# One Silu over both halves of the gate, one Softplus over both halves of dt, in a Mamba and 1-bit convolution kernel

## The reference, cut to what matters

```python
xz = jnp.einsum('bld,ed->ble', x, W_in)
xc, z = jnp.split(xz, 2, axis=-1)
xt = conv_general_dilated(jnp.transpose(xc, (0, 2, 1)), conv_w, ...)   # 4 taps, per channel
xc = silu(jnp.transpose(xt, (0, 2, 1)) + conv_b)
dbc = jnp.einsum('ble,re->blr', xc, W_x)                               # 8 rows of dt, 16 of B, 16 of C
dt = softplus(jnp.einsum('blr,er->ble', dbc[..., :8], W_dt) + b_dt)
# for each step: h = exp(dt * A) * h + (dt * xc) * B;   y = sum over states of h * C
y = (y + xc * D_skip) * silu(z)
return jnp.einsum('ble,de->bld', y, W_out)
```

## Time and profile before

| | us |
|---|---|
| median of 3 runs | 813.15 |
| lowest and highest run | 813.04, 813.65 |
| the profiled execution | 812.14 |
| its span | 810.3 |

### The profile page before, as it was taken

One profiled execution on the slowest core, in us unless ns is written; L12 is line 12 of the kernel. 1 busy time (PEld: TensorE's weight loads), 2 busy tenths in 40 slices (PEclk: granted clock), 3 DMA queues, 4 the chain that ended last, 5 costly groups with the idle time before them and its releaser, 6 DMA issues.

```text
span 810.3 us, 13741 instructions
## 1 busy us (share of the span) xinstructions
PE 740.5 (91%) x4854; PEld 403.1 (50%) x4854; DVE 727.1 (90%) x488; ACT 724.0 (89%) x1358; POOL 690.5 (85%) x211
## 2 busy tenths in 40 slices
PE   8798989898989898998989898989898997899998
PEld 5544444444444444544444544444544444557876
DVE  4799999999999999999999999999999999995141
ACT  5899999999999999999999999999999999865050
POOL 0579999999999999999999999999999999970000
PEclk9999999999999999999999999999999999999999
DMA  7817071726252433516161616253533525000011
GB/s 209 299 32 267 12 248 53 243 86 224 78 200 103 181 123 124 205 58 234 31 232 56 243 57 225 105 202 100 186 117 113 191 59 198 35 2 1 0 40 66
DMA packets 40173, 106.05 MB, mean 131 GB/s; under 512 B 8012, under 2 KB 11176, under 8 KB 40104
## 3 DMA queue, kind: packets, MB, share of 16 engines
q1 hardware_dynamic: 38476, 104.87, 37.2%
q10 hardware_dynamic: 1628, 0.30, 0.2%
HBM read 102.01 MB, written 3.15 MB: 130 GB/s over the span
## 4 chain that ended last, share of the span: by engine, by line
PE 34%; ACT 31%; DVE 14%; issue 11%; POOL 8%; DMA 2%; ACTq 1%; POOLq 0%; DVEq 0%; SPq 0%
PE bank L1261 11%; ACT product L772 10%; DVE state L1030 9%; PE bank L1547 8%; ACT bank L741 6%; ACT state L752 6%; PE bank L1254 5%; PE bank L1240 5%; POOL state L648 3%; POOL state L659 3%; DVE bank L1030 3%; PE bank L1365 2%; ACT xc L787 2%; ACT L860 2%; ACT L870 1%
## 5 line engine op out<-in xcount | busy, mean ns | idle before, releaser
L659 POOL TENSOR_TENSOR state<-state,wide 128x2048 f32<-128x2048 f32 (+1 forms) x104 | 408.1, 3956 | 5.4 <-DVE state L1030 5.4
L648 POOL TENSOR_TENSOR state<-u,wide 128x1024 f32<-128x1024 f32 (+1 forms) x77 | 249.1, 3259 | 25.3 <-DVE state L997 24.3
L1261 PE MATMUL bank<-state,ident 64*64 64x512 f32 x2048 | 250.1, 601 | 7.4 <-POOL state L659 7.4
L772 ACT ACTIVATE product<-u_tok,b_tok 128x256 f32<-128x256 f32 x588 | 248.0, 499 | 3.0 <-PE bank L1254 2.9
L1030 DVE TENSOR_TENSOR_SCAN state<-bank,state 128x1024 f32<-128x1024 f32 x109 | 246.7, 2276 | 3.3 <-ACT bank L741 2.2
L752 ACT ACTIVATE state<-dt,a_neg 128x512 f32<-128x512 f32 x294 | 193.0, 711 | 0.0
L1254 PEld LDWEIGHTS bank<-ident,product 128*128 128x128 f32 x1176 | 129.4, 141 | 121.0 <-issue 100.2
L1254 PE MATMUL bank<-ident,product 128*128 128x128 f32 x1176 | 156.0, 276 | 27.8 <-DVE state L1030 19.9
L1030 DVE TENSOR_TENSOR_SCAN bank<-state,bank 128x1024 f32<-128x1024 f32 x77 | 173.9, 2277 | 3.0 <-PE bank L1254 3.0
L1030 DVE TENSOR_TENSOR_SCAN state<-state,bank 128x1024 f32<-128x1024 f32 x70 | 158.4, 2267 | 3.2 <-PE bank L1254 3.2
L741 ACT ACTIVATE bank<-dt,a_neg 128x512 f32<-128x512 f32 x218 | 140.7, 677 | 0.9 <-DVE state L1030 0.2
(11 more groups left out here) (103 smaller groups left out, 469.0 us busy)
## 6 DMA issues: line engine op xcount, KB each, us to landing
wide<-bc_rows SPq DMA_DIRECT2D x159, 512.0 KB, 5.8
wide<-bc_rows SPq DMA_DIRECT2D x47, 256.0 KB, 3.9
x_t<-in_x_dram SPq DMA_DIRECT2D x4, 512.0 KB, 6.0
out_dram<-x_t SPq DMA_DIRECT2D x8, 256.0 KB, 2.0
k_room<-in_L_conv_w_dram SPq DMA_DIRECT2D x2, 576.0 KB, 6.7
bc_rows<-dbc SPq DMA_DIRECT2D x32, 32.0 KB, 1.5
state<-in_L_conv_W_in_dram SPq DMA_DIRECT2D x2, 256.0 KB, 3.8
x_tok<-in_x_dram ACTq DMA_DIRECT2D x1, 256.0 KB, 3.7
```

Of the source, the lines that this page charges most:

```text
L648: pool.tensor_tensor(tiles(group), u_for(len(group)), rows(b_wide, PLAIN.index(s), len(group)), ALU.mult).then_inc(plain_input, 1)
L659: pool.tensor_tensor(tiles(group), tiles(group), rows(c_wide, group[0] % NST, len(group)), ALU.mult).then_inc(output_pool, 1)
L772: act.activation(product[j % PRODUCTS][:, blk, :], u_tok[:, blk, :], ACT.Identity, scale=b_tok[k % 2][:, blk, s:s + 1]).then_inc(product_r ...
L1261: return pe.matmul(y_sum[64 * h:64 * h + 64, b, :], weights[rows, :], source[rows, h, :], start=first, stop=last)
```

## The change

The two ACTIVATEs of `gates` become one over 128 x 1024, read from both banks of z; the two of `make_dt` become one, also over 128 x 1024, which has no bias operand. b_dt comes in by the matmul instead: `w_dt_raw` gets a column behind each of its two copies of W_dt, so that the turned weights have nine rows, and the ninth row of `dbc` is 1. That 1 is made by `copy_dbc`, which becomes an Identity with a bias of one column, `one_row`, that is 1 on the partitions of the two ninth rows and 0 elsewhere. The waits on the gate and on dt are on whole tiles now.

```diff
-VECTORS = 3
+VECTORS = 2
...
-            for v, name in enumerate(("conv_b", "b_dt", "D_skip")):
+            for v, name in enumerate(("conv_b", "D_skip")):
...
             for row in (BC, 64 + BC):
                 eng.dma_start(w_dt_raw[m][:, :, row:row + RANK],
                               t[f"L0_conv_W_dt{m + 1}"].rearrange("(a p) r -> p a r", p=128)).then_inc(load_small[m], 16)
+                eng.dma_start(w_dt_raw[m][:, :, row + RANK:row + RANK + 1],
+                              t[f"L0_conv_b_dt{m + 1}"].rearrange("(a p u) -> p a u", p=128, u=1),
+                              allow_slow_non_contiguous=True).then_inc(load_small[m], 16)
...
-        SMALL_LOADS = 16 * (2 + VECTORS + 2)
+        SMALL_LOADS = 16 * (2 + VECTORS + 4)
...
+            pool.wait_ge(identities, 2)
+            pool.tensor_tensor(one_row[:, :], ident[:, XROWS:XROWS + 1], ident[:, 64 + XROWS:64 + DROWS],
+                               ALU.add).then_inc(one_ready, 1)
...
-            def gates(k, h):
+            def gates(k):
 
                 wait(act, gated, HALVES * (k - 1))
-                wait(act, z_mm, 2 * k + h + 1)
-                act.activation(gate[k % 2][:, h, :], z_place(k)[h], ACT.Silu).then_inc(gate_ready, 1)
+                wait(act, z_mm, HALVES * (k + 1))
+                z = banks[:, 0:HALVES, :] if k == 0 else banks[:, 6:6 + HALVES, :]
+                act.activation(gate[k % 2][:, :, :], z, ACT.Silu).then_inc(gate_ready, 1)
...
+                if k == 0:
+                    act.wait_ge(one_ready, 1)
                 wait(act, rows_stored, 32 * k)
-                copy(dbc[:, :], work[0][:, 0:THALF]).then_inc(dbc_ready, 1)
+                act.activation(dbc[:, :], work[0][:, 0:THALF], ACT.Identity, bias=one_row[:, 0:1]).then_inc(dbc_ready, 1)
...
-                for h in range(HALVES):
-                    wait(act, dt_mm, 2 * k + 2)
-                    act.activation(dt[m][:, h, :].rearrange("p (a n) -> p a n", a=2),
-                                   banks[:, 6:8, THALF * h:THALF * (h + 1)], ACT.Softplus,
-                                   bias=b_dt[m][:, h:h + 1]).then_inc(dt_ready, 1)
+                wait(act, dt_mm, 2 * k + 2)
+                act.activation(dt[m][:, :, :].rearrange("p h (a n) -> p h a n", a=2),
+                               banks[:, 6:8, :].rearrange("p a (h n) -> p h a n", h=HALVES),
+                               ACT.Softplus).then_inc(dt_ready, 1)
...
                 if k > 0:
-                    wait(pe, gate_ready, 2 * k + 1)
+                    wait(pe, gate_ready, k + 1)
...
-                        if h == 0 and a == 1:
-                            wait(pe, gate_ready, 2 * k + 2)
-                        rows = slice(64 * a + BC, 64 * a + XROWS)
+                        rows = slice(64 * a + BC, 64 * a + DROWS)
```

More of the change, by code:

```diff
@@ L148, in mamba_conv_kernel @@
         eps = sb("eps", [128, 1])
+        one_row = sb("one_row", [128, 1])
         least = sb("least", [128, 1])
@@ L161, in mamba_conv_kernel @@
         XROWS = BC + RANK
-        TROWS = 64 + XROWS
+        DROWS = XROWS + 1
+        TROWS = 64 + DROWS
         THALF = CHUNK // 2
@@ L179, in mamba_conv_kernel @@
         vectors = [sb(f"vectors{m}", [128, VECTORS * HALVES]) for m in range(2)]
-        conv_b, b_dt, d_skip = ([vectors[m][:, HALVES * v:HALVES * v + HALVES] for m in range(2)]
+        conv_b, d_skip = ([vectors[m][:, HALVES * v:HALVES * v + HALVES] for m in range(2)]
                                 for v in range(VECTORS))
@@ L258, in mamba_conv_kernel @@
         twin_ready = sem("twin_ready")
+        one_ready = sem("one_ready")
         a_exp = sem("a_exp")
@@ L664, in make_u @@
                 m = k % 2
-                wait(pool, dt_ready, HALVES * (k + 1))
+                wait(pool, dt_ready, k + 1)
                 wait(pool, xc_ready, 2 * k + 2)
@@ L826, in _ @@
             make_xc(0, 0)
-            gates(0, 0)
-            gates(0, 1)
+            gates(0)
             act.wait_ge(load_k, K_LOADS)
@@ L865, in _ @@
                     skip_diagonal()
-                gates(k + 1, 0)
-                gates(k + 1, 1)
+                gates(k + 1)
                 products(n + 12)
@@ L937, in _ @@
                 dve.memset(w_dt_raw[m][:, :, 0:BC], 0.0).then_inc(zeros, 1)
-                dve.memset(w_dt_raw[m][:, :, XROWS:64 + BC], 0.0).then_inc(zeros, 1)
+                dve.memset(w_dt_raw[m][:, :, DROWS:64 + BC], 0.0).then_inc(zeros, 1)
             dve.memset(x_t[:, :, 0:LPAD], 0.0).then_inc(zeros, 1)
@@ L983, in first_u @@
                 dve.wait_ge(xc_ready, 2)
-                dve.wait_ge(dt_ready, HALVES)
+                dve.wait_ge(dt_ready, 1)
                 dve.tensor_tensor(u[:, :, :], dt[0][:, :, :], xc[0][:, :, :], ALU.mult).then_inc(u_ready, 1)
@@ L1046, in post @@
                 wait(dve, summed, NST * (k + 1))
-                wait(dve, gate_ready, 2 * k + 2)
+                wait(dve, gate_ready, k + 1)
                 if b >= 2:
@@ L1229, in project @@
                 if part == 0:
-                    wait(pe, dt_ready, HALVES * k)
+                    wait(pe, dt_ready, k)
                     wait(pe, res_added, outputs_before(k - 1))
@@ L1320, in turn_b @@
             def turn_b(k):
-                wait(pe, dt_ready, HALVES * (k + 1))
+                wait(pe, dt_ready, k + 1)
                 for blk in range(BLOCKS):
```

## The result

| | before | changed |
|---|---|---|
| median of 18 runs, us | 812.5 | 816.09 |
| lowest and highest | 811.59, 814.55 | 812.97, 819.34 |
| the profiled execution | 812.14 | 819.34 |
| its span | 810.3 | 817.5 |

The changed kernel is slower: the ratio is 1.0043, 95% interval 1.0034 to 1.0052, which is 3.6 us between the medians. The forecast was 3.5 us (816.65, on the 813.15 of three earlier runs). But the runs of the changed kernel spread over 6.4 us and those of before over 3.0, and the profiled execution is the slowest of the 18, 7.2 us above the one of before. So the first question to the trace is where 7.2 us come from, the second why the median shows half of it.

A forecast was written before the change was run, and what follows sets the result against it. GpSimd was taken to set the pace, ScalarE close behind, after a start set by W_dt's landing. Landing 3.2, longer `copy_dbc` 0.1 and later `project_dbc` 0.2 gave +3.5 us: 813.15 to 816.65, own range 814.5 to 819, widened down to 813.4.

The forecast's parts named there:

- GpSimd sets the pace and ScalarE's saving is lost on it: Steady stretch: GpSimd paces items at 43.37 us, so ScalarE's 0.20 us saved per item, 3.0 in all, counts nothing.
- ScalarE will wait more for u: Steady stretch: ScalarE's wait for the turned u grows from 2.6 us by up to 3.0 us.
- step 4: What waits longer: the whole gate needs both halves of z, so ScalarE starts it up to 0.3 us later.
- TensorE is 0.3 us late at `project_dbc` and takes it back: Each item: `project_dbc` waits for the whole gate, about 0.3 us; TensorE's 3.4 us free per item absorbs it.
- +0.2: First pass of the loop: TensorE has no gaps, so the later `project_dbc` costs 0.2 us, bounds 0 and 0.4.
- The loads decide, and by the landing: Start: b_dt's 512 small packets delay the shared semaphore, and the landing moves by 2 us or more; chance 0.69.
- The size of the landing: Start: W_dt and b_dt land 3.2 us later, between bounds of 1.3 and 5.3 us.
- It all goes into the end: Start: the whole 3.2 us reaches the end, since the small groups' turning and all behind it wait for one semaphore.
- The rule on bundles: Rival on b_dt's loads: small packets pass in bundles, landing 1.5 us later, total 814.95 us; chance 0.14.
- the middle estimate: b_dt's loads: engines alternate queues packet by packet, so 32 small packets each wait 0.112 us, 3.6 us in all.

The follow-up runs named there:

- both pairs with and without the change: Changed against before, both with W_dt's own semaphore and later turning: 811.60 against 810.83 us; with GpSimd also relieved: 806.88 against 807.03 us.
- own wait: W_dt (and b_dt's columns, if changed) on its own semaphore, turned behind `project_dbc`: 811.60 us on the changed kernel, 810.83 on the one before.
- less on GpSimd: Both kernels with W_dt's own semaphore and later turning, half of state 13 left unmultiplied on GpSimd: changed 806.88 us, before 807.03.
- the 14 transposes: Changed kernel with 14 idle transposes on TensorE between the first taps and the small groups' turning: 814.56 us, ratio 1.0024.
- 34 transposes: Changed kernel with 34 idle transposes on TensorE in the wait for the loads: 814.70 us, ratio 1.0033 against the kernel before.
- the repeated one: Changed kernel as it is, timed again beside the kernel before: 816.27 us, ratio 1.0043.
- b_dt as rows: Changed kernel with b_dt loaded as contiguous 1 KB rows on their own semaphore, issued ahead of W_dt: 815.04 us, ratio 1.0024.

## Why the prediction was right, and where its sum was not

- *GpSimd sets the pace and ScalarE's saving is lost on it.* Right. The period stayed (43.37, 43.35), relieving GpSimd alone made both kernels faster, and both pairs with and without the change end level. ScalarE's list did get shorter: from the first xc to the first decay after dt it was 447.66 - 437.94 = 9.72 us and is 455.62 - 446.06 = 9.56, so 0.16 saved where 0.20 was summed. Gate and dt take 1025 and 1024 ns (1020 forecast, so the four-run source costs nothing), dbc 459 (475).
- *ScalarE will wait more for u.* Not so: 2.2 us instead of 2.6. The new wait of 0.9 us is for z, at the gate, which step 4 had.
- *TensorE is 0.3 us late at `project_dbc` and takes it back.* Right for the steady stretch: 0.30 us in the brackets above. In the first pass +0.2 was charged. With the same start in both (own wait), the first u came at 59.42 against 59.25, +0.17, but the second at 103.42 against 103.60: the pass after it gave 0.35 back. The pair with less on GpSimd gives back 0.34 there. The term should have been about -0.2.
- *The loads decide, and by the landing.* Right, shown from both sides (columns removed, columns added alone) and by the kernel that loads them and doesn't wait.
- *The size of the landing.* 3.2 us was summed. The semaphore came 2.8 and 3.8 us later in two profiled executions of the changed kernel (2.3 with the 14 transposes), and in the two pairs that don't wait the packets ended 2.7 and 2.9 us later. So this term was about right.
- *The term that was missing.* "It all goes into the end" was right as far as it goes, but more goes with it: while TensorE waits for the landing its clock falls, and 3.1 us are lost on the three blocks behind. Nothing in the sum held that. The profiled execution was 7.2 us slower, twice the forecast; the repeated one was 6.1 above the 812.35 of before. Where 34 transposes kept the clock up, the turning was 3.1 us later than before and the profiled execution 2.5 us slower. The median of 3.6 lies between such cases. That it came within 0.1 us of the 3.5 forecast is luck: no trace shows an execution that costs 3.5.
- *The rule on bundles.* The Trainium skill (DMA: Bandwidth & Descriptors, "Queues, rings and completion order") has an engine take a bundle of descriptors from one queue before it turns to the next. I worked out 1.5 us by that rule, and this was wrong in itself: SP's queue would send bundles too, so two turns would wait for two bundles of SP's, which is 2 x 9 to 2 x 17 packets of 0.112 us, 2 to 3.8 us as an estimate from that page's figures and the earlier trace rows. The size of the landing does not tell this from single turns, nor do the 50 packets of the earlier trace rows. The times of the packets do: 37 of those 50 lie singly between two of SP's, so the trace disagrees with the page here, and the middle estimate had the right mechanism.
- *What was missed in the kernel before.* Its own start waited for W_dt, 0.59 us in its trace. I read the chain and saw the DMA, and priced only what would be added to it. Read as an offer, it is worth more than the change: 1.4 us in the median by the own wait alone. That is more than the wait of the one trace; where the rest comes from is not shown.

## What to carry to other kernels

When an operand moves from one form to another, count what its load becomes: 256 rows of one number are 256 packets, and 512 of them beside a long transfer on another queue landed about 3 us late here, and held back whatever shared their semaphore. Give small loads a semaphore of their own, issue the ones that are needed first first, and put their wait where the data is used. And a wait ahead of TensorE costs more than its length when it lets the clock fall; the matmuls behind it pay. A coincidence of totals, as here, is only found out when the trace is laid beside each term of the sum.

## What the runs showed of the hardware that I had not expected

- The granted clock was 0.50 for the 6 us after TensorE had idled from 11.15 to 15.89, and 3.1 us were lost on three blocks of matmuls. It stayed at 1.00 through these blocks when 34 transposes filled the gap, and also after a wait of 1.81 us (b_dt as rows). The Trainium skill (TensorE: Matmul & The Clock Gate, "The HAM clock gate (the 'warmup' mystery)") describes a gate that lets fewer clock pulses through to an engine that has had little to do of late; the trace agrees, with 0.50.
- The clock over a whole execution is no safe mark of this fall: it sorted the first 18 runs of the changed kernel and not the 11 of its repetition.
- Two DMA queues took turns packet by packet: 37 of 50 packets of 4 or 32 bytes lay singly between two long ones of the other queue.
- W_dt's last packet ended at 8.89, 11.22 and 12.23 us in three kernels that issued it from 3.26, 3.56 and 3.85 on; with the same issue time it differed by up to 0.9 us between executions.
- An ACTIVATE over 1024 columns of PSUM in four runs of 256 takes 1024 ns, the same as one in straight order, 1025 ns.
